# A graph network and a mixture of experts on one core: the experts' products up in native fp32 instead of in parts, and another order of the last products

## The reference, cut to what matters

```python
for e in range(NUM_EXPERTS):
    h = jax.nn.gelu(xg @ w1[e], approximate=False)
    y = jnp.where((bin_ids == e)[:, None], h @ w2[e], y)
w = expert_weights.reshape(-1)[order][:, None]
out = jnp.zeros((T, hs), x.dtype).at[token_ids].add(w * y)
```

## Time and profile before

| what | value |
|---|---|
| median of 3 runs | 164.88 us (164.72 to 165.08) |
| the profiled execution's own time | 164.8 us |
| its span in the profile | 163.1 us |
| PE busy | 146.3 us (90%) |
| DVE, ACT, POOL busy | 119.6, 82.6, 34.9 us |
| TensorE's granted clock, mean | 0.988 of full speed |

### The profile page before, as it was taken

How to read it: one execution, slowest core, us unless ns; L and a number is a source line. 1 busy time by engine, 2 the same in 40 slices (tenths; PEclk the granted TensorE clock), 3 DMA queues, 4 the chain that set the end, 5 groups by cost and what they waited for, 6 DMA issues and landing times.

```text
span 163.1 us, 3502 instructions
## 1 busy us (share of the span) xinstructions
PE 146.3 (90%) x1130; PEld 96.7 (59%) x1133; DVE 119.6 (73%) x300; ACT 82.6 (51%) x210; POOL 34.9 (21%) x55
## 2 busy tenths in 40 slices
PE   2978899999999999999999999998999999999800
PEld 1436677878889855746844445543777873777100
DVE  1899999999999969898567758899567745443300
ACT  3268667777777785302421615995354333533100
POOL 7310000000000000000000600047700876173650
PEclk9999999999999999999999999999999999999995
DMA  3999999999000000000000000424698598547585
GB/s 89 264 380 288 275 373 371 367 368 312 17 0 4 2 4 4 2 0 4 0 0 0 0 4 0 171 88 129 201 326 310 112 196 191 72 53 91 78 115 64
DMA packets 15354, 21.71 MB, mean 133 GB/s; under 512 B 2942, under 2 KB 7808, under 8 KB 15332
## 3 DMA queue, kind: packets, MB, share of 16 engines
q1 hardware_dynamic: 12994, 16.02, 29.3%
q0 software_dynamic: 2240, 5.24, 17.7%
q10 hardware_dynamic: 98, 0.17, 0.3%
HBM read 15.19 MB, written 6.23 MB: 131 GB/s over the span
## 4 chain that ended last, share of the span: by engine, by line
PE 61%; DVE 19%; issue 5%; POOL 4%; DMA 4%; ACT 1%; POOLq 1%; DVEq 0%
DVE ring L749 11%; PE bank L1670 10%; PE bank L1549 10%; PE bank L1887 7%; PE bank L1875 6%; PE bank L1524 4%; PE bank L1878 4%; DMA ring<-x_rows,from_i 2%; PE bank L1848 2%; POOL ring L656 2%; PE bank L1470 2%; PE bank L1808 2%; PE bank L1514 2%; DVE stats L1085 2%; DVE x_sb L1079 2%
## 5 line engine op out<-in xcount | busy, mean ns | idle before, releaser
L1549 PE MATMUL bank<-ring 128*128 128x110 bf16 x324 | 30.0, 222 | 3.7 <-DVE ring L749 2.3
L749 DVE TENSOR_TENSOR ring<-iota_slots,lo 128x1024 bf16<-128x1024 f16 (+1 forms) x41 | 27.4, 669 | 0.0
L1549 PEld LDWEIGHTS bank<-ring 128*128 128x128 bf16 x324 | 19.7, 98 | 11.6 <-issue 5.9
L1261 ACT CAST at<-bank 128x400 f32 (+1 forms) x41 | 20.6, 502 | 7.5 <-PE bank L1555 6.6
L749 DVE TENSOR_TENSOR ring<-iota_dst,key 128x880 bf16<-128x880 f16 (+1 forms) x41 | 24.4, 595 | 0.0
L653 POOL CAST at_r<-ew 128x1024 fp32r<-128x1024 f32 x2 | 2.6, 1328 | 82.6 <-PE bank L1799 82.6
L667 POOL DMA_INDIRECT out<-at,to_i x10 | 15.7, 1572 | 20.7 <-DMA out<-x_sb 8.0
L1782 PE MATMUL bank<-wd3t_sb,at 128*128 128x512 f32 x40 | 17.7, 592 | 0.0
L1670 PE MATMUL bank<-at,ring 128*128 128x512 bf16 (+1 forms) x89 | 16.8, 343 | 0.1
L656 POOL DMA_INDIRECT ring<-x_rows,from_i x10 | 11.4, 1135 | 17.3 <-DMA x_rows<-at 14.5
L1887 PE MATMUL bank<-ew,at 128*128 128x512 f32 x32 | 14.9, 594 | 0.0
(11 more groups left out here) (223 smaller groups left out, 246.5 us busy)
## 6 DMA issues: line engine op xcount, KB each, us to landing
ew<-in_w SPq DMA_DIRECT2D x16, 512.0 KB, 9.5
x_sb<-in_x SPq DMA_DIRECT2D x9, 256.0 KB, 5.4
out<-x_sb SPq DMA_DIRECT2D x9, 256.0 KB, 4.1
wd3t_sb<-in_Wd3T SPq DMA_DIRECT2D x1, 512.0 KB, 4.8
x_rows<-xn SPq DMA_DIRECT2D x1, 512.0 KB, 2.8
x_rows<-at SPq DMA_DIRECT2D x1, 512.0 KB, 2.8
w1t_sb<-in_W1T SPq DMA_DIRECT2D x1, 256.0 KB, 5.0
bd_sb<-in_bd SPq DMA_DIRECT2D x1, 256.0 KB, 4.1
```

The costliest lines, as they stand in the source:

```text
L749: last = v.tensor_tensor(hot[:, slot, 0:tiles].rearrange("p t (n a) -> p t n a", a=2), lanes[:, 0:n].rearrange("p (n a) -> p n a", a=2).un ...
L1261: nc.scalar.copy(at[:, :, bass.ds(column, wide)], bank[j][:, 0:CH * wide].rearrange("p (c n) -> p c n", c=CH)).then_inc(s_placed, 1)
L1549: last = mm(to, hot_src[:, j, t], hot_dst[:, j, t], start=(t == 0 and not ends), stop=(first and t == tiles - 1), skip_group_check=not ends)
```

## The change

What it does: PE makes the product up as eight native fp32 products of 160 columns per expert, straight from `ew1` and the transposed tokens, which are now kept once (ACT keeps the first half and the tails, DVE the second half). Nothing is split: L653, L1051, L1060, L1410, L1107, L1111, L1418 and L1121 have no counterpart on the branch `sparse`. Gelu reads PSUM. Both halves `m` of an expert lie in one bank (2 or 3 by turns), and `s_up_sp` counts one for an expert, not two. In the last part of the order, the product down of expert 6 stands ahead of the product up of expert 7, and the second team's tails ahead of the product down of expert 7; POOL adds in that order too.

```diff
+        def of_up(e):
+            return bank[2 + e % 2][:, 0:KF * SLOTS].rearrange("p (k t) -> p k t", k=KF)
...
                 for c in range(TC - 1, REACHED):
                     sp.wait_ge(s_x2, c + 1)
-                    sp.wait_ge(s_up_sp, c - TC + 2)
+                    sp.wait_ge(s_up_sp, (c - TC + 3) // 2)
...
-            for e in range(2):
-                nc.gpsimd.tensor_copy(w1_first[e], weights(e)[0]).then_inc(s_whi, 1)
...
-                for e in range(NE):
+                for e in range(NE - 1):
                     add_to_tokens(e)
                     if e + XG + 2 < NE:
                         gather(e + XG + 2)
                     if (e + 1) % TEAM == 0:
                         add_tails(e // TEAM)
+                add_tails(TEAMS - 1)
+                add_to_tokens(NE - 1)
...
+                def keep_gathered(e):
+                    if e >= 2:
+                        dve.wait_ge(s_up_sp, e - 1)
+                    dve.wait_ge(s_xgT, 2 * e + 2)
+                    v.tensor_copy(xg_t[:, e % 2, 2:4, 0:P],
+                                  bank[1][:, 0:2 * P].rearrange("p (k t) -> p k t", k=2)).then_inc(s_xg_dve, 1)
...
-                for e in range(2, NE):
-                    first_part(e)
...
+                def finish_tails(e):
+                    q = e % TEAM * MORE
+                    nc.scalar.activation(hs_tail[:, e // TEAM, :, q:q + MORE], of_up(e)[:, :, P:], ACT.Gelu).then_inc(s_hs_tail, 1)
+
+                def finish_hidden(e):
+                    act.wait_ge(s_up_sp, e + 1)
+                    if e >= 2:
+                        act.wait_ge(s_down_sp, e - 1)
+                    nc.scalar.activation(hs[:, e % 2], of_up(e)[:, :, 0:P], ACT.Gelu).then_inc(s_hs, 1)
...
                     for m in range(KF):
-                        acc = bank[2 + m]
                         for k in range(KD):
-                            mm(acc[:, 0:2 * SLOTS], w1_hi[:, k, m * P:(m + 1) * P],
-                               xg_t[:, e % 2, k].rearrange("p h t -> p (h t)"), start=(k == 0), stop=False)
-                        for k in range(KD):
-                            last = mm(acc[:, 0:SLOTS], w1_lo[:, e, k, m * P:(m + 1) * P], xg_t[:, e % 2, k, 0],
-                                      start=False, stop=(k == KD - 1))
-                        last.then_inc(s_up_sp, 1)
+                            last = mm(of_up(e)[:, m], ew1[:, e, k, m * P:(m + 1) * P], xg_t[:, e % 2, k], start=(k == 0),
+                                      stop=(k == KD - 1))
+                    last.then_inc(s_up_sp, 1)
...
                 for e in range(NE):
-                    if e + 1 < NE:
+                    if e + 2 < NE:
                         up_slots(e + 1)
-                    if e + 2 < NE:
                         transpose_gathered(e + 2)
...
+                    if e == NE - 1:
+                        down_tails(TEAMS - 1)
                     down_slots(e)
-                    if (e + 1) % TEAM == 0:
+                    if e + 2 == NE:
+                        up_slots(e + 1)
+                    if (e + 1) % TEAM == 0 and e + 1 < NE:
                         down_tails(e // TEAM)
```

More of the change, by code:

```diff
@@ L235, in gnn_moe @@
         hs = at2_flat[:, 4 * NP:4 * NP + 2 * KF * P].rearrange("p (b k t) -> p b k t", b=2, k=KF)
-        w1_first += [xnt_r[:, o * w1_len:(o + 1) * w1_len] for o in range(2)]
         x2_more = at2_flat[:, 3 * NP:3 * NP + 2 * D].rearrange("p (b n) -> p b n", b=2)
@@ L703, in _ @@
                         add_tails(e // TEAM)
+                add_tails(TEAMS - 1)
+                add_to_tokens(NE - 1)
             with pool.If(dense != 0):
-                for e in range(2):
-                    nc.gpsimd.tensor_copy(weights_hi(e)[1], weights(e)[1]).then_inc(s_whi, 1)
-                for e in range(2, NE):
+                pool.wait_ge(s_ew, 16 * 2 * NE)
+                pool.wait_ge(s_agg2, len(SPANS))
+                for e in range(NE):
                     if e >= W_HI:
@@ L1045, in _ @@
             add_bias(CH - 1, CH)
[L1047 to L1051, removed]
             def weights_rest(e):
[L1055 to L1060, removed]
+                dve.wait_ge(s_whi, 2 * (e + 1))
+                for lo, w, hi in zip((up_lo(e), down_lo(e)), weights(e), weights_hi(e)):
+                    v.tensor_tensor(lo, w, hi.bitcast(F32), ALU.subtract).then_inc(s_wlo, 1)
             def hidden_rest(i):
@@ L1099, in _ @@
                                         ALU.add).then_inc(s_xn2_more, 1)
-                if TC - 1 <= c <= TC:
-                    weight_rest_of(c - TC + 1, 0)
             with dve.If(sparse != 0):
[L1103 to L1122, removed]
+                def keep_gathered(e):
[4 more added lines that the diff above has]
+                                  bank[1][:, 0:2 * P].rearrange("p (k t) -> p k t", k=2)).then_inc(s_xg_dve, 1)
                 def keep_results(e):
@@ L1398, in keep_gathered @@
                     if e >= 2:
[L1399 to L1418 removed]
+                        act.wait_ge(s_up_sp, e - 1)
+                    act.wait_ge(s_xgT, 2 * e + 1)
+                    nc.scalar.copy(xg_t[:, e % 2, 0:2, 0:P],
+                                   bank[0][:, 0:2 * P].rearrange("p (k t) -> p k t", k=2)).then_inc(s_xg_act, 1)
+                    act.wait_ge(s_tailT, e // TEAM + 1)
+                    nc.scalar.copy(xg_t[:, e % 2, :, P:], of_tails(e)).then_inc(s_xg_act, 1)
+                def finish_tails(e):
[6 more added lines that the diff above has]
+                    nc.scalar.activation(hs[:, e % 2], of_up(e)[:, :, 0:P], ACT.Gelu).then_inc(s_hs, 1)
                 def keep_tails(g):
@@ L1429, in _ @@
                 act.wait_ge(s_slot_weight, 1)
-                for e in range(2, NE):
-                    first_part(e)
                 keep_gathered(0)
                 keep_gathered(1)
-                keep_part(0)
                 for e in range(NE):
-                    act.wait_ge(s_hs_sum, KF * (e + 1))
-                    if e >= 2:
-                        act.wait_ge(s_down_sp, e - 1)
-                    nc.scalar.activation(hs[:, e % 2], hs_raw[:, :, 0:P], ACT.Gelu).then_inc(s_hs, 1)
-                    q = e % TEAM * MORE
-                    nc.scalar.activation(hs_tail[:, e // TEAM, :, q:q + MORE], hs_raw[:, :, P:], ACT.Gelu).then_inc(s_hs_tail, 1)
+                    finish_hidden(e)
+                    finish_tails(e)
                     if e + 2 < NE:
                         keep_gathered(e + 2)
-                    if e + 1 < NE:
-                        keep_part(e + 1)
                     if e % TEAM == 0 and e:
@@ L1901, in down_tails @@
                     last.then_inc(s_down_more, 1)
+                pe.wait_ge(s_ew, 16 * 2 * NE)
                 transpose_gathered(0)
```

63 lines of the change are left out of this document (16 added, 47 removed).

## The result

The changed kernel takes 165.96 us (median of nine runs, 165.29 to 166.51); the kernel before, beside it, 164.88. The ratio is 1.0062, 95% interval 1.0047 to 1.0078: slower by 0.6%. Two more sets of runs of the same kernel, each beside the kernel before, gave 1.0018 (1.0001 to 1.0035) and 1.0038 (1.0024 to 1.0052), so the loss is 0.2 to 0.6%, 0.3 to 1.0 us. The kernel before itself took 164.88, 165.53, 165.37 and 164.68 us in the four sets of runs: 0.5% between sets, and ratios from different sets are that much less sure beside each other. The profiled execution took 165.64 us with a span of 163.9; that of before 164.8 and 163.1.

The account below looks back on a forecast made before the run. PE was taken to bound the kernel until a closing chain of POOL adds and landings. Span 163.1 + 0.25 (order) + 1.33 (product up) − 0.93 (gathers) = 163.75 us, time 165.4 us, range 164.1 to 166.9.

Parts of the forecast that it names:

- The gathers: POOL's gathers, freed of DVE's subtractions, each take 0.95 us, so all experts start 0.93 us earlier on PE.
- The product up: PE's 16 native records of 0.144 us per expert make 2.30 us, 0.19 more than before; +1.33 us over seven.
- My lower end: Product up on PE at 0.134 us a record, scaled from 256 columns: +0.04 us per expert, 0.3 over seven.
- My upper end: Product up on PE at 2.64 us per expert: +0.53 us each, 3.7 over seven.
- The new order: End of POOL's add chain: expert 6's add comes earlier, but one more add follows the tails': +0.25 us.
- the removed DVE sum: DVE's sums of hidden parts were taken as hidden behind PE's work, so their removal gives nothing.
- The stores: Stores of chunks 5 and 6 move POOL's first add by less than 1 us; effect on the time: nothing.
- PE's wait for gelu: PE idle some 0.7 us between expert 7's product up and the tails.
- Cheap records: Rival: native 160-column records on PE cost only 0.134 us, shift 0.3 instead of 1.33, time 164.4 us; chance 0.20.
- Short landings: Rival: the two last add landings take 4.7 us each; time 164.5 us; chance 0.13.
- Long gathers: Rival: the gathers on POOL stay long, the 0.93 us is lost, time 166.4 us; chance 0.17.
- binding weight loads: Rival: weight loads bind on PE, a record costs 0.165 us, 3.7 instead of 1.33, time 167.8 us; chance 0.08.

Follow-up runs that it names:

- experiment 1: Changed kernel with the order of products and adds put back as before, native products kept: 164.19 us, ratio 0.993 to the kernel before.
- Experiments 5: experiment 1 plus three unused DVE subtractions of 1024 elements, both inputs in SBUF, ahead of the sums of chunks 6 to 8: ratio 0.998.
- experiment 6: experiment 1 plus three unused DVE multiplications by 1.0 of 1024 elements, one SBUF input, ahead of the sums of chunks 6 to 8: ratio 0.9929.
- experiment 9: experiment 1 plus three unused DVE pieces, each two subtractions of 512 elements with one SBUF and one PSUM input: ratio 0.9959.
- experiments 4: Changed kernel without expert 7's add, its part of the output left out: 163.65 us, ratio 0.9908 to the kernel before.
- experiment 7: The changed kernel itself, unaltered, measured a second time beside the kernel before: ratio 1.0018.
- experiment 11: The changed kernel itself, unaltered, measured a third time beside the kernel before: ratio 1.0038.
- experiment 8: Changed kernel without expert 5's add, its part of the output left out: 164.8 us, ratio 1.0011 to the kernel before.
- experiment 2: Products up in parts as in the kernel before, with the changed kernel's new order of last products and adds: 168.69 us, ratio 1.0194.
- experiment 3: Changed kernel with the tails last on PE and POOL; expert 6's product down still ahead of expert 7's product up: 163.95 us, ratio 0.9908.

## Why the prediction was right, and where it was not

The direction was right: 165.4 us forecast, 165.96 measured in the first set, 0.3% more. In the profile the forecast span was 163.75 and the measured 163.9. But the split behind the sum was wrong. By its terms the arithmetic alone loses (+1.33 - 0.93 = +0.40 us) and the order hardly costs (+0.25). In the profile the arithmetic gains (+0.42 - 0.97 = -0.55) and the order costs 1.35, and experiment 1 shows the gain of the arithmetic by itself. That the sum came out is luck. Point by point:

- **The gathers** (0.93 us). Right in the cause and the size. Expert 1's transposes start 0.97 us earlier, the gathers take 1.14, 0.98, 0.96 us. The first has some 0.2 us of its own even with DVE idle, which I had put at nothing. Experiments 5, 6 and 9 show the cause. The pace was not PE's, though: I had expert 1's rows land at 114.1, counted from the end of their gather, and they landed at 114.81. In the profiles in which PE waits for them, their transposes start 3.70 to 3.84 us behind the start of the third gather, whether it took 0.96 us on POOL or 1.41; what the change won is that it starts 1.04 us earlier (111.04 against 112.08). Where PE does set the pace (experiments 4 and 7), the gain is 1.2 us.
- **The product up** (0.144 us a record, 2.30 us, +1.33 us over seven). This is the term that was mis-sized. It measured 0.136, 2.17 us, +0.42 us over seven. The error was the straight line between 129 and 256 columns. The rows of native fp32 of 64 columns, which I had not set beside the others, show it, in the timeline of PE of the kernel before:

```profile
79.30 1.00 PE L1703 MATMUL bank<-w2t_sb,xnt 128*128 128x64 f32 x8
80.14 0.56 PE L1730 MATMUL bank<-chosen_value,ring 128*128 128x40 bf16 x16
```

  64 columns cost (80.14 − 79.30)/8 = 0.105 us, 129 cost 0.121, and 160 now 0.136. From 64 to 129 columns the cost rises by 0.016 us only, and from 160 on it follows the columns (0.136/160 and 0.215/256 are within 2%). The bend lies somewhere below 160 columns, and a line drawn across it reads too high. My lower end, 0.134, was the better reading, and the rival built on it (164.4 us, faster) was wrong only in that it left the end of the program at +0.25 us. My upper end, 2.64 us, took for a record the 0.165 us of a product of 320 columns of the reduced type; no run shows a native record of 160 columns at that cost, and the changed kernel's took 0.136.
- **The new order** (+0.25 us). The mechanism was right: the tails' add starts on the landing of expert 6's, at 155.60 against 155.6 forecast, and expert 7's follows 1.85 us later. The size was not. With the two other terms at what they measured, 163.1 + 0.42 − 0.97 = 162.55, so in this profile the order costs 1.35 us. Set against native products in the old order on the same chip (with idle DVE work, as that is what ran there) it is 1.0018 to 0.9929 (experiments 7 and 6) and 1.0038 to 0.9959 (11 and 9), 0.8 to 0.9%, 1.3 to 1.5 us. Three parts of it were too small, 1.10 us together. The landing of expert 6's add I took from before, 5.16 us, where it was followed by another; now it follows expert 5's by 1.85 us and takes 5.68 us until the tails' add starts (6.2 in experiment 11, 5.0 alone in experiment 8): 0.52 us. Expert 6's add starts at 149.92 instead of 150.02 + 0.42 - 0.97 = 149.47, 0.45 us, nearly all of it because it queues behind expert 5's: that one, kept by DVE at 146.18 + 0.75 = 146.93, starts 1.14 us later, not 0.76 as before; experiment 1 has the same 1.14 us (DVE at 145.76, add at 147.65). What this wait is stays open. The last 0.14 us are behind expert 7's add, 6.45 us instead of 5.16 + 1.15. (The last add of before, which I called alone, was not quite: expert 7's of 153.95 took 5.4 us to land by the profile, so it was under way until 159.3.)
- **Two errors of opposite sign** (-0.91 for the product up, +1.10 for the order, and -0.04 for the gathers) so made a sum within 0.15 us. The forecast was right by that: had the product up been read at 0.136 and the order left at +0.25, the sum would have said 163.1 + 0.25 + 0.42 − 0.93 = 162.84 us of span, 0.3 us faster.
- **The rest.** ACT's and DVE's removed work beyond the gathers moved nothing on PE that the profile shows: PE has no idle time among the experts before or after. But I put the removed DVE sum at nothing, and under the new order it isn't: that DVE is free to keep expert 6's result at 147.90, as the forecast's 149.98 for its add takes for granted, is due to it (experiment 2, section 1 of the experiments). The stores cost nothing: POOL's first add still waits for them, at 125.00 against 126.52, and no add at the end hangs on it. PE's wait for gelu is 0.59 us (0.7 forecast) and costs nothing, as the landing comes later.
- **The rivals.** Cheap records came true (0.136 us) without making it faster. Short landings (4.7 us) didn't come; the opposite did, 5.68 us from expert 6's add to the tails'. Long gathers didn't come (1.14, 0.98, 0.96 us), nor did a record of 0.165 us, which binding weight loads were to show.

## What to carry to other kernels

When a chain of dependent DMAs ends a kernel, count what is left behind the last wait for a landing, not how early the wait ends: here 1.65 us won ahead of it were paid back by 2.8 us for the second add behind it. Try each half of a double change alone: the native products were worth 0.4 to 0.7%, the order cost 0.8 to 0.9%, and a third order of the same work (experiment 3) keeps the gain. When an order is changed on one engine, read the written order of every engine that takes its results: in experiment 2 DVE's unchanged order undid what PE's was to win. To price an instruction of a size that the trace doesn't have, lay three or more sizes side by side and look for the bend before drawing a line.

## What was not expected of the hardware

- A multiplication of 1024 fp32 elements from SBUF to SBUF took 0.69 us on DVE, against 1.22 us for the subtraction of two inputs, and a gather that started beside it ended 0.82 to 0.84 us behind its end, as with the slower one.
- An indirect add of 128 rows took 4.75 us to land alone and 5.92 us 1.9 us behind another (both in experiment 8); the tails' add, which waits for such a landing, starts up to 0.8 us apart in profiles of one kernel (experiments 7 and 11).
- Native fp32 of 160 columns costs hardly more than the three products of reduced type did (2.17 against 2.11 us per expert), and it needs no parts.
